# A graph layer and a top-2 mixture of experts on one core: the experts' second layer as fp32 products instead of f16 halves

## The reference

```python
agg = jnp.zeros_like(x).at[dst].set(x[src])        # the last edge of a target wins
h = jnp.concatenate((x, agg), axis=-1)             # x: the layer norm of the input
x = x + (h @ W.T + b)
tokens = layernorm(x)
probs = softmax(tokens @ router_w.T); rw, re = top_k(probs, 2); rw = rw / rw.sum(-1)
combine = zeros((N, 8)).at[arange(N)[:, None], re].set(rw)
out = tokens
for e in range(8):
    h = gelu(tokens @ w1[e] + b1[e], approximate=False)
    y = h @ w2[e] + b2[e]
    out = out + combine[:, e:e + 1] * y
return x + out
```

## Time and profile before

| | us |
|---|---|
| median of 3 runs | 1001.22 |
| lowest, highest | 999.37, 1004.05 |
| span of the profiled execution | 1180.7 |

### The profile page before, as it was taken

How to read it: one execution, slowest core, us unless ns; L and a number is a source line. 1 busy time by engine, 2 the same in 40 slices (tenths; PEclk the granted TensorE clock), 3 DMA queues, 4 the chain that set the end, 5 groups by cost and what they waited for, 6 DMA issues and landing times.

```text
span 1180.7 us, 28647 instructions
## 1 busy us (share of the span) xinstructions
PE 836.3 (71%) x9319; PEld 702.9 (60%) x9319; DVE 868.3 (74%) x1893; ACT 630.4 (53%) x1669; POOL 484.9 (41%) x527
## 2 busy tenths in 40 slices
PE   1599888887666862243444468888888888888886
PEld 1588887776555651132333256776766666767766
DVE  6999999995677764477688946776667666766666
ACT  3466666663444331264553345666666565666665
POOL 7000000004445556764650035555555555555554
PEclk9799999999888795555555789999999999999999
DMA  8800000003664444553551712222222222222220
GB/s 228 266 28 27 27 27 27 27 27 84 208 202 149 118 121 144 156 165 99 160 170 63 7 42 68 64 65 61 65 66 64 64 65 66 63 67 65 70 60 11
DMA packets 79211, 104.89 MB, mean 89 GB/s; under 512 B 22593, under 2 KB 64538, under 8 KB 78994
## 3 DMA queue, kind: packets, MB, share of 16 engines
q0 software_dynamic: 21408, 54.87, 16.6%
q1 hardware_dynamic: 57714, 48.76, 14.8%
HBM read 63.16 MB, written 44.01 MB: 91 GB/s over the span
## 4 chain that ended last, share of the span: by engine, by line
PE 31%; DVE 28%; issue 14%; another core or an unknown queue 12%; ACT 8%; DMA 3%; POOL 1%; ACTq 1%; DVEq 1%; SPq 1%; POOLq 0%
PE bank L983 12%; PE bank L997 9%; DVE arena L1099 7%; PE bank L786 6%; DVE arena L1082 5%; ACT arena L750 2%; PE bank L951 2%; PE bank L809 1%; ACT arena L711 1%; DVE bst L1300 1%; DVE arena L1283 1%; DVE big L1297 1%; POOL arena L517 1%; ACT arena L695 1%
## 5 line engine op out<-in xcount | busy, mean ns | idle before, releaser
L983 PE MATMUL bank<-arena,w1s 128*128 128x128 f16 x3000 | 211.2, 220 | 78.0 <-issue 69.1
L983 PEld LDWEIGHTS bank<-arena,w1s 128*128 x3000 | 177.8, 98 | 112.8 <-issue 109.8
L505 POOL DMA_INDIRECT arena<-key_rows,cid x98 | 94.8, 968 | 330.0 <-DVEq L1215 252.7
L750 ACT ACTIVATE arena<-bank,b1s 128x128 f32<-128x128 f32 x500 | 142.0, 368 | 155.6 <-remote 152.1
L532 POOL DMA_INDIRECT out<-arena,gidx x125 | 140.3, 1123 | 188.9 <-DVE arena L1438 149.5
L997 PE MATMUL bank<-w2s,arena 128*128 x1500 | 184.1, 272 | 1.4 <-DVE arena L1418 0.7
L521 POOL DMA_INDIRECT arena<-tok_rows,gidx x125 | 124.4, 995 | 107.4 <-DVE gidx L1407 69.4
L809 PE MATMUL bank<-wgs,arena 128*128 128x256 f16 x1176 | 160.0, 289 | 5.6 <-issue 5.4
L1433 DVE SCALAR_TENSOR_TENSOR arena<-bank,arena 128x256 f32<-128x256 f32 x125 | 60.1, 481 | 132.7 <-remote 129.5
L997 PEld LDWEIGHTS bank<-w2s,arena 128*128 128x128 f16 x1500 | 140.7, 98 | 17.8 <-issue 1.7
L809 PEld LDWEIGHTS bank<-wgs,arena 128*128 128x128 f16 x1176 | 121.7, 104 | 34.1 <-issue 8.6
(11 more groups left out here) (215 smaller groups left out, 1414.9 us busy)
## 6 DMA issues: line engine op xcount, KB each, us to landing
agg_rows<-arena SPq DMA_DIRECT2D x49, 256.0 KB
tok_rows<-arena SPq DMA_DIRECT2D x13, 896.0 KB
big<-x SPq DMA_DIRECT2D x5, 1792.0 KB, 14.1
arena<-w SPq DMA_DIRECT2D x16, 256.0 KB, 2.9
big<-x SPq DMA_DIRECT2D x6, 512.0 KB
arena<-tok_rows,gidx POOLq DMA_INDIRECT x125
out<-arena,gidx POOLq DMA_INDIRECT x125
arena<-key_rows,cid POOLq DMA_INDIRECT x98
```

The source lines that it names most:

```text
L505: gp.indirect_dma_start(er[:, b % 2, s, :], None, key_rows, bass.IndirectOffsetOnAxis(cid[:, t:t + 1], 0)).then_inc(er_full[b % 2], 16)
L750: last = sc.activation(h32[:, u % 2, at:at + P], bank[2 + u % 2][:, at:at + P], ACT.Gelu, bias=b1s[:, ds(e[x], 1), f], scale=1.0 / SCALE)
L983: last = mm(bank[2 + u % 2][:, at:at + P], parts[x, w, c, f], a[:, u % 4, c * P:(c + 1) * P], start=(n == 0), stop=(n == 5))
```

## The change

- `tile_out`: for each expert and each half of the hidden features one product whose stationary operand is gelu's fp32 row (`h32`) and whose moving operand is 256 columns of fp32 weights: four products a tile.
- `high_hidden` and `low_hidden`, and the tiles `hh` and `hl`, go. `h32` has four buffers; `gelu(j)` waits for `tile_out(j-4)` where it waited for `low_hidden(j-1)`; `tile_out` waits for `gelu` where it waited for `low_hidden`.
- `w2s` is two fp32 tiles of the same bytes. Its eight matrices are loaded straight into them, two transfers each, with a semaphore of their own; the edge keys use the same bytes as before. Staging, `high_weight` and `low_weight` remain for `w1` alone.
- The factor 64 of the second layer goes, and with it the scaling of `b2t` on ACT and the division of the gates.

The diff (the declarations of two semaphores are left out):

```diff
@@ -100,7 +100,7 @@
 
         big = sb("big", [P, T * D * 4], u8)
         w1s = [[sb(f"w1s{w}{c}", [P, E, D], f16) for c in range(2)] for w in range(2)]
-        w2s = [[sb(f"w2s{w}{c}", [P, E, D], f16) for c in range(2)] for w in range(2)]
+        w2s = [sb(f"w2s{c}", [P, E, D], f32) for c in range(2)]
         wgs = sb("wgs", [P, 2, 2, 2 * D], f16)
         rws = sb("rws", [P, 2, E], f32)
         b1s = sb("b1s", [P, E, 2], f32)
@@ -246,9 +246,7 @@
         xg = four.take([P, DEPTH, ROW], f32)
         xth = four.take([P, 4, 2 * P], f16)
         xtl = four.take([P, 4, 2 * P], f16)
-        h32 = four.take([P, 2, 4 * P], f32)
-        hh = four.take([P, 4, 4 * P], f16)
-        hl = four.take([P, 4, 4 * P], f16)
+        h32 = four.take([P, 4, 4 * P], f32)
         ob = four.take([P, DEPTH, D], f32)
 
         bank = [ctx.enter_context(nc.psum_tensor(f"bank{i}", [P, 512], f32)) for i in range(8)]
@@ -300 @@
         block = ctx.enter_context(nc.Block())
         x_chunk = 2 * B
-        keys = [w2s[w][c].rearrange("p e d -> p (e d)").bitcast(i32)[0:KP, 0:KR * 2 * CH]
-                for w in range(2) for c in range(2)]
+        keys = [w2s[c].rearrange("p e d -> p (e d)").bitcast(i32)[0:KP, n * E * D // 2:n * E * D // 2 + KR * 2 * CH]
+                for n in range(2) for c in range(2)]
 
         def key_part(rows, q):
             return rows[q * KP * KR:(q + 1) * KP * KR, :].rearrange("(p r) c -> p (r c)", r=KR)
@@ -412,7 +409,15 @@
                 store_agg(i, i % 2)
             for i in range(IB + 1, IB + 2 * E - 1):
                 m = i - IB + 1
-                store_and_load(i, i % 2, (w1, w2)[m // E], m % E)
+                if m < E:
+                    store_and_load(i, i % 2, w1, m)
+                else:
+                    store_agg(i, i % 2)
+                if m == E:
+                    sp.wait_ge(s_keys, 64)
+                if m >= E:
+                    for c in range(2):
+                        sp.dma_start(w2s[c][:, m - E, :], w2[m - E, c * P:(c + 1) * P, :]).then_inc(s_w2, 16)
                 c = i - IB - 1
                 if c == 0:
                     sp.wait_ge(zeroed, 1)
@@ -422,7 +427,7 @@
                 store_agg(i, i % 2)
 
 
-            sp.wait_ge(w_prep, 2 * E)
+            sp.wait_ge(w_prep, E)
             sp.wait_ge(cid_ready, 1)
             sp.wait_ge(agg_stored[0], 16 * (T // 4 + 1))
             sp.wait_ge(agg_stored[1], 16 * (T // 4))
@@ -681,10 +686,7 @@
             act_pair(ND - 1, (ND - 1) % 2)
             for m in range(E):
                 act_pair(ND + m, (ND + m) % 2, groups=False, ws=w1s, e=m)
-            act.wait_ge(s_keys, 64)
-            for m in range(E, 2 * E):
-                act_pair(ND + m, (ND + m) % 2, groups=False, ws=w2s, e=m - E)
-            for d in range(ND + 2 * E, T // 2 + LAG):
+            for d in range(ND + E, T // 2 + LAG):
                 act_pair(d, d % 2, groups=False)
 
             def copy_transposed(m):
@@ -696,10 +698,6 @@
 
             m = 0
             for n, (first, more) in enumerate(PIECES):
-                if n == 2:
-                    act.wait_ge(s_b2, 16)
-                    flat = b2t.rearrange("p e d -> p (e d)")
-                    sc.activation(flat, flat, ACT.Copy, scale=SCALE).then_inc(b2_scaled, 1)
                 act.wait_ge(var_ready, T // 2 - PA + n + 1)
                 sc.activation(std[:, first:first + more], mv[:, first:first + more, 1], ACT.Sqrt,
                               bias=eps[:, :]).then_inc(std_ready, 1)
@@ -729,25 +727,20 @@
                               scale=pone[:, :]).then_inc(onval_ready, 1)
 
             act.wait_ge(tab_ready, 1)
-            act.wait_ge(b2_scaled, 1)
+            act.wait_ge(s_b2, 16)
 
             def high_tokens(i, u):
                 wait_tile(act, xd_ready, i, u, 1)
                 wait_tile(act, h_ready, i, u, -3)
                 sc.activation(xth[:, u % 4, :], bank[u % 2][:, 0:2 * P], ACT.Copy).then_inc(xth_ready, 1)
 
-            def high_hidden(i, u):
-                wait_tile(act, gelu_ready, i, u, 1)
-                wait_tile(act, y_ready, i, u, -3)
-                sc.activation(hh[:, u % 4, :], h32[:, u % 2, :], ACT.Copy).then_inc(hh_ready, 1)
-
             def gelu(i, u, e):
                 wait_tile(act, h_ready, i, u, 1)
-                wait_tile(act, hl_ready, i, u, -1)
+                wait_tile(act, y_ready, i, u, -3)
                 for x in range(2):
                     for f in range(2):
                         at = (2 * x + f) * P
-                        last = sc.activation(h32[:, u % 2, at:at + P], bank[2 + u % 2][:, at:at + P], ACT.Gelu,
+                        last = sc.activation(h32[:, u % 4, at:at + P], bank[2 + u % 2][:, at:at + P], ACT.Gelu,
                                              bias=b1s[:, ds(e[x], 1), f], scale=1.0 / SCALE)
                 last.then_inc(gelu_ready, 1)
 
@@ -758,8 +751,6 @@
                               bias=xg[:, u, D + 1:D + 2], scale=xg[:, u, D + 2:D + 3]).then_inc(bias_ready, 1)
 
             def act_step(i, u, j, known):
-                if j is None or 0 <= j - 1 < NT:
-                    high_hidden(*tile(i, u, -1))
                 if j is None or j + 2 < NT:
                     high_tokens(*tile(i, u, 2))
                 if j is None or 0 <= j < NT:
@@ -942,7 +933,8 @@
                 last.then_inc(on_used, 1)
 
             pe.wait_ge(tab_ready, 1)
-            pe.wait_ge(w_prep, 2 * E)
+            pe.wait_ge(w_prep, E)
+            pe.wait_ge(s_w2, 32 * E)
 
             def tile_in(i, u):
                 wait_tile(pe, xtl_ready, i, u, -1)
@@ -965,10 +957,9 @@
             def second_layer(e):
                 parts = {}
                 for x in range(2):
-                    for w in range(2):
-                        for c in range(2):
-                            parts[x, w, c] = w2s[w][c][:, ds(e[x], 1), :].rearrange("p a d -> p (a d)")
-                            pe.lower_ap(parts[x, w, c])
+                    for c in range(2):
+                        parts[x, c] = w2s[c][:, ds(e[x], 1), :].rearrange("p a d -> p (a d)")
+                        pe.lower_ap(parts[x, c])
                 return parts
 
             def tile_hidden(i, u, parts):
@@ -986,16 +977,13 @@
                 last.then_inc(h_ready, 1)
 
             def tile_out(i, u, parts):
-                wait_tile(pe, hl_ready, i, u, 1)
+                wait_tile(pe, gelu_ready, i, u, 1)
                 wait_tile(pe, o_ready, i, u, -1)
                 for x in range(2):
                     to = bank[4 + u % 2][:, x * D:(x + 1) * D]
-                    n = 0
                     for c in range(2):
-                        for a, w in ((hh, 0), (hl, 0), (hh, 1)):
-                            at = (2 * x + c) * P
-                            last = mm(to, a[:, u % 4, at:at + P], parts[x, w, c], start=(n == 0), stop=(n == 5))
-                            n += 1
+                        at = (2 * x + c) * P
+                        last = mm(to, h32[:, u % 4, at:at + P], parts[x, c], start=(c == 0), stop=(c == 1))
                 last.then_inc(y_ready, 1)
 
             def pe_step(i, u, j, known):
@@ -1189,8 +1177,8 @@
                 if d - LAG - 1 >= IB:
                     add_self(d - LAG - 1, (d - LAG - 1) % 2)
                 m = d - ND - 1
-                if 0 <= m < 2 * E:
-                    low_weight(m, m % 2, (w1s, w2s)[m // E], m % E)
+                if 0 <= m < E:
+                    low_weight(m, m % 2, w1s, m)
                 if d < T // 2:
                     if d < PA:
                         early_reciprocal(d, d % 2)
@@ -1328,7 +1316,7 @@
             ve.tensor_tensor(is1, q1, q2, ALU.is_gt)
             ve.tensor_tensor(is2, q1, q2, ALU.is_lt)
             dve.wait_ge(lexp_ready, 1)
-            step(ve.tensor_scalar(dv, e2v, 1.0, SCALE, ALU.add, ALU.mult))
+            step(ve.tensor_scalar(dv, e2v, 1.0, None, ALU.add))
             ve.reciprocal(rv, dv)
 
             dve.wait_ge(counts_ready, 1)
@@ -1412,11 +1400,6 @@
                 ve.tensor_tensor(xtl[:, u % 4, :], bank[u % 2][:, 0:2 * P], xth[:, u % 4, :], ALU.subtract
                                  ).then_inc(xtl_ready, 1)
 
-            def low_hidden(i, u):
-                wait_tile(dve, hh_ready, i, u, 1)
-                wait_tile(dve, y_ready, i, u, -3)
-                ve.tensor_tensor(hl[:, u % 4, :], h32[:, u % 2, :], hh[:, u % 4, :], ALU.subtract).then_inc(hl_ready, 1)
-
             def second_bias(i, u, e):
                 wait_tile(dve, bias_ready, i, u, 1)
                 ve.scalar_tensor_tensor(ob[:, u, :], b2t[:, ds(e[1], 1), :].rearrange("p a d -> p (a d)"),
@@ -1439,12 +1422,10 @@
                                         ALU.mult, ALU.add).then_inc(o_ready, 1)
 
             dve.wait_ge(tab_ready, 1)
-            dve.wait_ge(b2_scaled, 1)
+            dve.wait_ge(s_b2, 16)
 
             def dve_step(i, u, j, known):
```

(9 more changed lines are left out.)

## The result

| | before, us | changed, us | ratio (95% interval) |
|---|---|---|---|
| first measurement | 1000.3 (4 runs) | 1045.88 (4 runs) | 1.0459 (1.0427 to 1.0490) |
| second, another group | 999.94 (9 runs) | 1046.46 (5 runs) | 1.0462 (1.0437 to 1.0488) |

The changed kernel is 4.6% slower. Forecast were 1040 us and a range of 1012 to 1062 us.

A forecast was written before the change was run, and what follows sets the result against it. PE was taken to bound the expert step before and after; 44 us more for fp32 products less 5 us of preparation on the 1001 us median gave 1040 us, with a range of 1012 to 1062 us for 8 in 10.

The forecast's parts named there:

- PE bounds the step before: Expert stage: PE alone needs 2.86 us a step, longer than DVE's 2.51 and ACT's 2.46 us.
- the 2.92 us: Expert step assumed for timed runs before, PE bound with a little loss; other stages giving back 64 us would make 2.91.
- The price of the fp32 products: Second layer on PE: four fp32 products take 1.72 us for twelve f16 ones' 1.31 us, 0.41 us more a step.
- The rival of uncovered loads: Second layer on PE: eight fp32 weight loads stand alone, 1.0 us a tile, 125 us in all, 1165 us; chance 0.04.
- Relief of ACT and DVE worth nothing: Expert stage: ACT and DVE steps fall to about 1.93 and 1.91 us, worth nothing while PE sets the step.
- Preparation: Node stage: dropping the second weights' ACT and DVE preparation saves 5 us, between 0 and 6.7 us.
- The sum: Whole kernel: 44 us more in the expert stage less 5 us of preparation, 39 us more.
- the expert stage's term: Expert stage: step from 2.92 to 3.27 us, 0.35 us over 125 tiles, 44 us more.
- The 179.5 us between the span and the timed runs: Profile's span over the timed median, read with the "remote" waits as time that timed runs mostly do not have.
- The bounds on the step: Expert step of timed runs before: at least PE's 2.86 us, at most 3.43 us, the stage giving back at least 51.

The follow-up runs named there:

- e2_no_halves: Kernel before with gelu writing f16 high halves directly, both half computations removed and PE's work kept the same: 998.99 us, ratio 0.9985.
- e5_sixteen: Kernel before with a fourth f16 product, low half times low half, in each second-layer group, sixteen products a tile: 1048.0 us, ratio 1.0469.
- e1_products_only: Changed kernel with the high and low halves computed and waited for as before, though nothing reads them: 1046.36 us, ratio 1.0451.
- e0_before: Kernel before, unchanged, profiled a second time: 1000.59 us, ratio 1.0005, span 999.0 us.
- e8_after: Changed kernel, unchanged, run again in another group: 1046.46 us, ratio 1.0462 to the kernel before.

## Why the prediction was right

- **PE bounds the step before.** Right: 2.87 us in the median, 2.86 us as read off, shown by `e2_no_halves` (nothing gained without the halves) and `e5_sixteen` (all of PE's addition is paid). The mean of 2.94 us is near the 2.92 us that was taken, and that is luck: the 2.92 us came from a guess that the other stages would give back half of their bound. The loss is ten long steps, and they do not survive in a slower kernel.
- **The price of the fp32 products.** 1.78 us against 1.72 us forecast. The spacing of two matmuls of one product is 0.216 us as in the earlier trace rows; the rest is the head of the group. Of its eight matmuls the first is 436 ns long, the median 380 ns (all second-layer products: least/median/most):

```profile
L986 PE MATMUL bank<-w2s,arena x1000: 378/380/436, 625.7 to 1038.0; 128*128 x167
```

  From its start to the next it is 0.27 us. The likely reason, which no run tests, is that the load behind it, 0.19 us, has no long matmul before it to hide under: the products ahead of the group have 128 columns. This was priced at nothing, with 0.1 us as the worst case; it is about 0.056 us, 7 us in all. The eight loads otherwise disappear under the matmuls: they run for 1.60 us, inside the 1.78 us of the group.

```profile
853.01 1.60 PEld L986 LDWEIGHTS bank<-w2s,arena 128*128 128x128 f32 x8
```

  The rival of uncovered loads is not what this kernel shows: these loads and matmuls use the whole array (128*128), and they overlap. The rule of the Trainium skill's "TensorE: Matmul & The Clock Gate", Part 3, that loads overlap matmuls in flight only when they go to other row groups, does not hold here. The rival was also priced too low: its 0.12 us is the spacing of loads that already ran beside matmuls, while one load takes 0.19 us, which would make 1.5 us a tile.
- **Relief of ACT and DVE worth nothing.** Right as far as the timed runs tell: by `e1_products_only` to within 1 us in the changed kernel, by `e2_no_halves` within its interval in the kernel before.
- **Preparation.** 4.6 us by experiment, 5 us forecast. In the profiles the four batches with second weights take 38.3 us before and 34.3 us after.
- **The sum.** +48.3 us in the expert stage (44 forecast) and -2.5 us before it (-5 forecast) give +45.8 us plus a tail 0.4 us longer: the spans differ by 46.2 us, the times by 45.6 us. The forecast was 39 us, and in this pair of profiles both terms erred to the same side. But the start of the expert stage scatters. It lies at 621.5, 624.6 and 623.0 us in the three profiles with the old preparation (`e0_before`, `e2_no_halves`, `e5_sixteen`) and at 619.0, 617.6 and 619.6 us in the three with the new one (changed, `e1_products_only`, `e8_after`): 4.3 us earlier in the mean, near the forecast of 5 us. What was too small is the expert stage's term, 0.35 us a step where the mean steps differ by 0.39 us, the fp32 group's head above all.
- **What was wrong.** The 179.5 us between the span and the timed runs were read as time that the profiled execution has and the timed ones have not. Timed runs of 1183 us exist, with these waits, so the profile shows a slower condition of the same program. The bounds on the step that were worked out from them held: 111.9 us less in the expert stage and 69.9 us less before it, where the forecast had guessed 115 and 64 us. In the slower condition the change seems to come out otherwise, as the kernel with the preparation put back does.

## What to carry to other kernels

Count an fp32 product of 256 columns as four f16 ones, 0.43 us: replacing three f16 products of halves by one fp32 product makes TensorE's part a third longer (1.31 us became 1.78 us here). It can pay only where something that it relieves is the bound, which no run here shows. Read which engine is back to back in one step of the timeline; relieving an engine that waits for it in every step gives nothing. When a profile's span and the timed runs of the same kernel disagree, profile it again before trusting the waits: the two may come from different conditions.

## What the runs showed of the hardware that was not expected

The same program takes 1000 us in some groups (19 and 9 runs) and 1183 us in others (17 and 11 runs), steadily within a group, at the same granted clock in the expert stage (1.00 and 0.99). Whether this is a matter of the chip stays open, since the record has the same chip number at both times. In the slower condition PE's first-layer products come in pieces in 48 of 125 tiles, with starts over 0.2 us apart inside the layer; in `e0_before` that happens in none. The first profile, timeline of PE:

```profile
908.45 0.45 PE L983 MATMUL bank<-arena,w1s 128*128 128x128 f16 x5 [0.34 <-issue]
909.20 0.50 PE L983 MATMUL bank<-arena,w1s 128*128 128x128 f16 x6 [0.30 <-issue]
```

ACT and DVE then sit idle for 2 to 4 us before PE's results reach them. Replacing the scattered indirect stores of POOL by plain ones of SP in tile order makes that vanish in the steady steps of the expert stage and takes 120 us off (1183 to 1063 us).
